# New order of the steps in every engine queue, and new places of the filler products, in a fused decoder layer

## The reference

```
x = x + attn(layernorm(x))      # conditioned gated delta rule, 16 heads of 16
x = x + xattn(layernorm(x), ctx)  # differential cross attention on 64 context tokens
x = x + ffn(layernorm(x))       # causal conv, 8 experts of which 2 count, rms norm, gelu FFN
```

```
Sd = gt * S;  kS = kt . Sd;  S = Sd + kt (bt (vt - kS));  ot = qt . S
```

## Time and profile before

| what | value |
|---|---|
| median of 3 runs | 1439.71 us (1438.2 to 1439.93) |
| the profiled execution's own time | 1441.35 us |
| its span, first to last instruction | 1439.6 us |
| PE busy | 1358.7 us (94%) |
| DVE busy | 1155.8 us (80%) |
| ACT busy | 902.9 us (63%) |
| POOL busy | 209.2 us (15%) |
| mean granted PE clock | 0.987 of full speed |

### The profile page before, as it was taken

One profiled execution on the slowest core, in us unless ns is written; L12 is line 12 of the kernel. 1 busy time (PEld: TensorE's weight loads), 2 busy tenths in 40 slices (PEclk: granted clock), 3 DMA queues, 4 the chain that ended last, 5 costly groups with the idle time before them and its releaser, 6 DMA issues.

```text
span 1439.6 us, 41035 instructions
## 1 busy us (share of the span) xinstructions
PE 1358.7 (94%) x17183; PEld 883.8 (61%) x17220; DVE 1155.8 (80%) x3060; ACT 902.9 (63%) x1735; POOL 209.2 (15%) x204
## 2 busy tenths in 40 slices
...
DMA packets 22783, 35.76 MB, mean 25 GB/s; under 512 B 1992, under 2 KB 18504, under 8 KB 22344
## 3 DMA queue, kind: packets, MB, share of 16 engines
...
...
## 4 chain that ended last, share of the span: by engine, by line
PE 79%; DVE 11%; ACT 7%; issue 3%; DMA 0%; POOL 0%; ACTq 0%; SPq 0%; DVEq 0%
PE bank L2134 15%; PE bank L2037 6%; PE bank L1818 6%; PE bank L1691 6%; PE four L1904 4%; PE bank L2073 4%; PE bank L2059 4%; PE bank L1745 3%; PE bank L1716 3%; PE four L1923 3%; PE bank L1820 2%; PE four L1716 2%; PE four L1948 2%; PE four L1868 2%; PE bank L1810 2%
## 5 line engine op out<-in xcount | busy, mean ns | idle before, releaser
L2134 PE MATMUL bank<-w_sb,cs 128*128 128x512 f32 x512 | 248.3, 604 | 1.7 <-ACT qkv L1046 0.5
L744 POOL TENSOR_TENSOR decayed<-state,pk 128x512 f32<-128x512 f32 x64 | 71.5, 1116 | 748.3 <-DVE state L1433 729.8
L2134 PEld LDWEIGHTS bank<-w_sb,cs 128*128 128x128 f32 x512 | 90.9, 189 | 88.6 <-issue 64.1
L1046 ACT ACTIVATE cs<-bank 128x512 f32<-128x512 f32 x112 | 66.9, 597 | 96.8 <-PE bank L1697 42.4
L991 ACT COPY cs<-bank 128x512 f32<-128x512 f32 x114 | 66.4, 583 | 68.7 <-PE bank L2059 68.7
L779 ACT ACT_TABLE_LOAD x82 | 105.2, 1283 | 1.4
L1291 DVE SCALAR_TENSOR_TENSOR qkv<-pre,l_sb,qkv 128x512 f32<-128x512 f32 x144 | 105.8, 779 | 0.0
L1745 PEld LDWEIGHTS bank<-c_sb 128*128 128x128 f32 x772 | 94.4, 195 | 10.5 <-issue 9.4
L1745 PE MATMUL bank<-c_sb 128*128 128x128 f32 x772 | 99.7, 281 | 0.0
L2037 PE MATMUL bank<-kbx,cs 32*128 32x256 f32 x464 | 97.7, 401 | 1.4 <-DVE cs L1522 0.7
L1630 DVE SCALAR_TENSOR_TENSOR cs<-cs,rwt 128x256 f32<-128x256 f32 x196 | 91.3, 501 | 6.9 <-ACT cs L1046 4.1
...
## 6 DMA issues: line engine op xcount, KB each, us to landing
...
```

The source lines that it names most:

```text
L2134: mm(dst, x1T[:, k, b * TB:b * TB + TB], ew[:, k, ep * 512:ep * 512 + 512], start=k == 0, stop=False)
```

## The change

No step, wait, buffer or transfer is changed. The tables are replaced, and so are the numbers in `KEEP`; rounds -2 and -1 take their order from a table of their own, "start". In the new file "start" and "head" hold the same lists. Filler products are now 4, 116, 72, 59 and 42 in rounds -2, -1, 0, 7 and 8. Cut to the lines that the prediction speaks of (entries of absent stages stand in the head and start tables too, and are skipped):

```diff
@@ turns @@
-                for half, name, *args in ORDERS["head" if i <= 0 else "last" if i == NI else "drain" if i == NI - 1 else "steady"][engine]:
+                for half, name, *args in ORDERS["start" if i < 0 else "head" if i == 0 else "last" if i == NI else "drain" if i == NI - 1 else "steady"][engine]:
@@ KEEP @@
-KEEP = {(-1, 1, "cond"): 109, (-1, 1, "db"): 9, (-1, 1, "sum", 0): 5, (-1, 1, "sum", 1): 8, (-1, 2, "gate", 0): 2, (-1, 2,
+KEEP = {(-1, 1, "cond"): 61, (-1, 1, "db"): 9, (-1, 2, "gate", 0): 3, (-1, 2, "rot"): 4, (-1, 2, "turn1", 0): 36, (-1, 2,
@@ head, pe @@
-        -pt.4 -turn2.0 -sc.5.0 sum.2 -pt.13 +gate.1 sum.3 grow +cond -moe.5 vturn -qx.1.0 raw.0 -sc.6.0 -mi -turn4.1
+        -moe.15 -sc.3.0 -pt.6 grow -moe.20 -qx.1.0 -moe.1 -wp.1.0 -moe.30 sum.2 +gate.1 sum.3 -asum.0 -turn2.0 -ffu.0
+        -pv.7 +cond -asum.1 -moe.19 -pw.1.1 -sc.1.1 -pt.1 vturn -sc.3.1 raw.0 raw.1 -wp.0.0 raw.2 -pt.2 -sc.5.0 raw.3
@@ head, dve @@
-        norm.0 -top.1.0 dsel.0 dsel.1 gsub.0 -av.1.0 norm.1 norm.2.0 norm.2.1 norm.3.0 -acc.5.1 -acc.12.0 -dconv.0.2
-        norm.3.1 gsub.1 am.0 am.1 am.2 -acc.10.1 -ln3.1.0 +cond am.3 solve.0.0 -dconv.1.0 -av.7.0 -max.0.0 solve.0.1
+        -av.1.0 -max.3.0 -av.3.1 -max.4.1 -ln2.0.0 -hnorm.0 norm.0 dsel.0 dsel.1 gsub.0 norm.1 gsub.1 norm.2.0
+        norm.3.0 norm.2.1 norm.3.1 -max.2.0 -dconv.0.2 am.0 -acc.10.0 am.1 +cond -max.3.1 am.2 am.3 -acc.1.1 -acc.7.1
...
-        -acc.3.1 onorm.0 -acc.6.0 -acc.7.0 -acc.8.0 onorm.1 og.0 -acc.6.1 *rot.1 *scan -wp.1 og.1 -acc.9.0 x1.0 -x1T.0
-        x1.1 *unrot.0 *unrot.1'''),
+        -acc.7.0 *rot.1 -acc.8.0 -acc.9.1 *scan onorm.1 og.0 *unrot.0 og.1 -acc.9.0 -max.4.0 *unrot.1 x1.0 -top.0.0
@@ head, act @@
-        -turn6.1 kx.0 -moe.25 -den.2 sq.2 -pt.8 -max.7 kx.2 -max.4 +gate.1 -moe.3 sq.3 -pt.3 +cond.0 dexp -moe.18 rs.2
-        rs.3 gexp.1 gexp.2 -moe.24 -moe.9 -moe.4 -moe.11 -turn2.0 -max.6 -den.3 -pt.15 kx.1 gexp.0 vturn -pt.6 kx.3
+        sq.2 -pt.13 -turn2.0 -pt.3 +gate.1 sq.3 kx.2 -moe.24 -asq.1 -ln3.1 -moe.18 -moe.3 -moe.2 rs.2 -moe.23 +cond.0
+        -turn6.1 -den.2 -pt.1 dexp -den.0 rs.3 gexp.0 -pt.4 -moe.6 -moe.19 gexp.1 gexp.2 -pt.15 -pt.8 kx.1 vturn
@@ steady, pe @@
-        grow sum.2 +gate.1 -turn2.0 -qx.0.0 sum.3 -qx.0.1 +cond -turn2.1 vturn -sc.0.0 -qx.1.0 -sc.0.1 -qx.1.1 raw.0
-        raw.1 -sc.1.0 -sc.1.1 -pt.0 raw.2 -pt.1 raw.3 -pv.0 raw.4 raw.5 -sc.2.0 -sc.2.1 -pt.2 raw.6 raw.7 -pt.3 -pv.1
+        +gate.1 grow -turn2.0 sum.2 sum.3 +cond -qx.0.0 -turn2.1 -qx.0.1 vturn -qx.1.0 -sc.0.0 -sc.0.1 -qx.1.1 raw.0
+        raw.1 -sc.1.0 -sc.1.1 -pt.0 raw.2 -pt.1 raw.3 raw.4 -pv.0 raw.5 raw.6 -pt.2 -sc.2.0 -sc.2.1 -pt.3 raw.7 -pv.1
...
-        -pt.10 +proj.3.0 -pt.11 z.1 -pv.5 cs.0.0 -sc.7.0 cs.0.1 -sc.7.1 -pt.12 z.2 d1.1 -pt.13 -pv.6 z.3 -asum.0
+        -pt.10 +proj.3.0 -pt.11 z.1 cs.0.0 -pv.5 cs.0.1 -sc.7.0 -sc.7.1 -pt.12 z.2 -pt.13 d1.1 -pv.6 z.3 -asum.0
...
-        -moe.29 cs.6.0 -moe.31 *turn1.1 -mo.0.0 -mo.0.1 *rot -turn5.1 cs.6.1 -mi -mo.1.0 -mo.1.1 d1.7 -turn6.0 cs.7.0
-        cs.7.1 -ffd.0 -turn6.1 co.0 co.1 -ffd.1 onorm.0 wo.0 onorm.1 *gate.0 -ffu.0 -ffu.1 +sum.0 wo.1 wo.2 +sum.1'''),
+        -moe.30 -moe.31 *turn1.1 -mo.0.0 -mo.0.1 cs.6.0 -turn5.1 -mi cs.6.1 -mo.1.0 -mo.1.1 d1.7 -turn6.0 cs.7.0
+        cs.7.1 -turn6.1 *rot -ffd.0 co.0 co.1 -ffd.1 -ffu.0 onorm.0 onorm.1 *gate.0 wo.0 -ffu.1 +sum.0 wo.1 wo.2
@@ steady, dve @@
-        m.7 -hnorm.1 o.6.0 o.6.1 o.6.2 o.6.3 s.7 o.7.0 o.7.1 o.7.2 o.7.3 *rot.1 *scan onorm.0 onorm.1 og.0 -top.0.1
-        og.1 -ffu.0 *unrot.0 -ffu.1 x1.0 x1.1 *unrot.1'''),
+        o.5.3 m.7 -hnorm.1 o.6.0 o.6.1 o.6.2 o.6.3 s.7 o.7.0 o.7.1 o.7.2 o.7.3 *rot.0 -ffu.0 *rot.1 *scan onorm.0
+        *unrot.0 onorm.1 og.0 og.1 -ffu.1 *unrot.1 x1.0 x1.1'''),
@@ steady, act @@
-        -moe.23 +silu.2 -turn5.0 +silu.3 -moe.16 kx.4 -moe.25 -moe.27 +silu.4 *turn1 -moe.29 -moe.31 +silu.5 -hnorm.0
-        *rot -moe.12 -moe.26 -turn5.1 -hnorm.1 -turn6.0 -ffd.0 osq.0 -turn6.1 -ffd.1 osq.1 onorm.0 onorm.1 +sq.0 +sq.1
+        -turn5.1 -hnorm.1 -turn6.0 +silu.4 +silu.5 -turn6.1 *rot kx.4 -ffd.0 -ffd.1 osq.1 onorm.0 onorm.1 +sq.0
@@ last, act @@
-        -pw.0 -ln3.1 mkq.2.1 -moe.1 -turn4.1 mkq.0.1 -moe.3 osq.1 -pw.1 -moe.5 kx.3 -top.0 dexp kx.0 -top.1 vturn
+        +proj.5 osq.1 -ln3.1 +silu.6 *ln1 -moe.1 mkq.7.1 -turn4.1 -moe.3 -top.0 -pw.1 kx.6 kx.0 +cond.1 kx.2 *gate.0
+        -moe.5 -top.1 mkq.3.1 -moe.7 -moe.9 -moe.11 -moe.6 kx.4 +brep.1 +silu.5 -moe.13 -moe.15 kx.1 -moe.17 mkq.3.0
```

373 lines of the change are left out of this document (210 added, 163 removed).

## The result

| | before | after |
|---|---|---|
| median | 1439.09 us (1438.2 to 1439.93, 4 runs) | 1377.58 us (1372.59 to 1378.43, 4 runs) |
| ratio | | 0.9559, 95% interval 0.9532 to 0.9586 |
| profiled execution | 1441.35 us, span 1439.6, clock 0.987 | 1372.59 us, span 1370.8, clock 0.999 |

What follows compares the result with a forecast made beforehand. PE, busy 94% of the span, was taken as the bound, partly with filler. Terms -9.4 - 8.0 - 1.0 - 3.4 - 7.2 - 2.0 = -31.0 took the median 1439.71 to 1409 us; own range 1403 to 1415, wider range 1397 to 1424.

Steps and rivals of the forecast that it cites:

- the start: Rounds -1 and 0 up to `ln2`: forecast to come 21.8 us earlier, with `ln2` of round 0 near 181.5.
- the middle and tail of round 0: Round 0 behind `raw.0`: 1 us from new filler places, 3.4 us from moved rotation and scan and removed fillers.
- -8.0: From round -1 into round 0, up to `raw.0`: `grow` first on PE and fewer fillers save 8.0 us (7.1 to 9.5).
- `cond` part: Round -1: filler products ahead of `cond` cut from 109 to 61, so it starts about 34.2 instead of 43.66, saving 9.4 us.
- the steady rounds, the term of -1.2 us each: Rounds 1 to 6: 2.5 us of PE waits saved less 1.3 us of cost, 1.2 us a round, 7.2 in six.
- three signs of being wrong: `cond` not started by 36, a full-clock steady round not shorter than 161.6, or more than three clock falls added.
- rival B: Steady rounds save 3 us each and two clock falls go: 1394, half of both 1401; chance 0.11.
- That is 2.2 us: Steady rounds: PE waits of `pv` for softmax copies (1.5 us) and `*rot` for its transpose (0.7) saved.
- Against it stands the tail.: End of steady rounds: moved silus, a table load and `*rot`'s copy on ACT delay `onorm` 0.9 us, one `wo` 1.3 us.
- Rounds 7 and 8, -2: Last two rounds: 2 us saved, taken near the middle of -10.3 (all PE idle time) and +4.7 (added fillers exposed).

Runs made afterwards that it cites:

- joined kernel: Kernel before, with the four split score pairs sc.u.0 and sc.u.1 (u = 0, 3, 4, 7) made neighbours in PE's steady order; 1418.7 us, ratio 0.986.
- the run with the old tail: Changed kernel with the steady steps behind the experts ordered as before on PE, DVE and ACT; 1398.6 us, 1386.4 at full clock.

## Why the prediction was wrong

**Right: the start, with some luck at its end.** Every step of it up to `ln2` of round 0 came within 1 us of its forecast, 22.7 us instead of 21.8. Up to `raw.0` this holds in a second profile of the changed kernel too (34.42, 80.95 and 91.61 us). `ln2` does not: the first profile had no fall of the clock before it, the kernel before had two in round 0, and the second profile of the changed kernel has falls at 84 to 94 and 122 to 134 us and reaches `ln2` 3.8 us later, 18.9 us ahead of before:

```profile
184.31 0.74 DVE L1256 BATCH_NORM_STATS2 stat<-xr 128x6 f32<-128x256 f32 x2
```

So part of the agreement on the middle and tail of round 0 is the clock's. The run with only the start new gives 18.8 (20.5 at full clock). That -8.0 is what it was forecast to be rests on the traces alone; only the `cond` part was run by itself, and gave 7 to 8 of its 9.4.

**Wrong: the steady rounds, the term of -1.2 us each.** Measured are -6.3 at full clock. None of the prediction's three signs of being wrong came up (`cond` started at 34.21, a steady round was shorter than 161.6, no falls were added): they guarded against too little gain, and the round came out below even rival B's 158.5. Three sentences of the prediction failed.

*"only 6.13 us of it are idle, and no order can save more than these in a steady round at this clock"*. This took PE's busy time as fixed by the list of instructions. It isn't: where two neighbours use different rows of PE, the order sets whether they overlap. This is the largest piece of a steady round that a run shows, 2.7 to 2.8 us, both ways. The rows that would have told could have been asked of the trace: the score group of the kernel before by shape (tile 32*128), and its timeline in groups of four and of eight. In the kernel before four pairs already ran joined, in 1.14 us.

*"`pv.1`, `pv.6` stand behind another step now and `*rot` behind `turn6.1`. That is 2.2 us"*. The wait of 1.5 us ahead of `pv` was real, and the order that shortens it to 0.4 made the joined kernel slower by 4.4 us at full clock. The length of a wait in the profile was not its price.

*"Against it stands the tail."* It was booked as a cost of 1.3 us a round, and the sign was wrong: added to the joined pairs and the new head, the new tail, without the silus, takes 0.9 us off a round. (The 14 us of the run with the old tail hold the wait named above.) The silus and their table load, 1.28 us a round, cost nothing where they were taken back alone (1377.1 against 1377.9 us). What moved: before, the rotation's first product (1.12 us) stood in DVE's queue inside the last pieces of the recurrence, and its scan (1.61 us) ahead of `onorm` with 1.12 us of waiting behind it; in the new table all of it stands behind `o.7`, where DVE would wait for the norm anyway. DVE at the end of round 2, before and after:

```profile
509.45 1.12 DVE L1247 TENSOR_TENSOR rota<-swapped,cosT 128x512 f32<-128x512 f32 x1
517.72 1.61 DVE L1259 TENSOR_TENSOR_SCAN rota<-rota,zc,rotb 128x128 f32<-128x128 f32 x4
520.45 0.69 DVE L1457 TENSOR_TENSOR M<-M,shared 128x512 f32<-128x512 f32 x1 [1.12 <-ACT shared L772]
```

```profile
482.50 0.68 DVE L1297 TENSOR_TENSOR rota<-swapped,cosT 128x512 f32<-128x512 f32 x1
484.51 1.61 DVE L1309 TENSOR_TENSOR_SCAN rota<-rota,zc,rotb 128x128 f32<-128x128 f32 x4
486.03 0.67 DVE L1507 TENSOR_TENSOR M<-M,shared 128x512 f32<-128x512 f32 x1
```

From the end of `o.7` to `x1.1` both take 9.9 us (517.08 to 526.98, 482.58 to 492.52). So the tail's own chain got neither longer, as forecast, nor shorter; the recurrence reached its end sooner, seen from the round's start, 145.3 us instead of 151.7. That the rotation's place is the cause of a share of that is a reading of the two traces and not shown.

**The clock.** The prediction had no fall of the clock gained in its forecast, only in rival B. The profile of before shows five falls, one in each of the rounds 3 to 7, and two short ones in round 0; the changed kernel's shows one short one in round 1. (The second row at 0.98 in the earlier trace rows, which the prediction takes for round 6, is round 7; round 6 has 0.98 as well.) By the clock line an estimated 6.4 us of the 61.5 are clock (12.1 us at 0.988 against 5.7 at 0.995). The profile of the joined pairs alone has none in rounds 2 to 6 either, but a long one in the drain round. The stretch of that fall, and the whole round:

```profile
1171.60:1188.70 17.10, 17.10 (x215) 13.90 (x215) 5.91 (x14) 7.32 (x19) 7.85 (x10) 0.51 0.27 43
1155.71:1315.55 159.84, 149.41 (x2041) 102.85 (x2045) 117.64 (x314) 89.12 (x177) 22.18 (x22) 0.94 0.07 16
```

159.84 us for a round that takes 153.26 in the kernel before. What makes the clock fall there wasn't found.

**Rounds 7 and 8, -2.** Measured -1.5, and +0.1 at full clock, which can't be told from nothing; the -2 was taken between two bounds and no run decides what it is made of. In the traces of before and after round 7 is at -3.7 (2.3 of it a fall of the clock) and round 8 at +1.0.

**Sum, at full clock.** Start -20.5, pairs -16.4, rest of the steady table -19.7 (-36.1 less -16.4), end +0.1: -56.5, and the clock -6.4: -62.9, against the measured -61.5. The prediction had -21.8, nothing, -7.2 and -2.0 for the four. *Open* stays how the -19.7 divide. Head and tail on the joined pairs give -7.7, taken out of the changed kernel +17.6 (with the extra wait in it), and the engines' middles gave their gain only as a set. Which wait or path the new middle takes away is not known.
